# Decoder layer on one core: ternary thresholds two batches later, first layer norm one batch earlier

## The reference, cut to what matters

```python
x = layernorm(x + attn(x, Wq, Wk, Wv, Wo))         # x: 16 batches x 112 tokens x 256
x = layernorm(x + xattn(x, ctx, Wq, Wk, Wv, Wout)) # ctx: 16 x 375 keys x 192, 8 heads of 128
x = layernorm(x + ffn(x, W1, b1, W2, b2))          # width 1024

def xattn(x, context, ...):      # each head: 1792 queries against all 6000 keys
    softmax(q @ k.T * 1.5 * 128 ** -0.5) @ v, then @ Wout + bout

def ternary(w):                                    # on W1 and W2, for ffn
    scale = maximum(mean(abs(w)), 1e-8)
    return clip(round(w / scale), -1, 1)
```

## Time and profile before

| | us |
|---|---|
| median of 3 executions | 2416.77 (2416.18 to 2417.38) |
| the profiled execution | 2416.18, its span 2414.4 |
| PE busy | 2301.5 (95%) |
| DVE busy | 2037.4 (84%) |
| ACT busy | 1870.8 (77%) |
| POOL busy | 1850.6 (77%) |

### The profile page before, as it was taken

How to read it: one execution, slowest core, us unless ns; L and a number is a source line. 1 busy time by engine, 2 the same in 40 slices (tenths; PEclk the granted TensorE clock), 3 DMA queues, 4 the chain that set the end, 5 groups by cost and what they waited for, 6 DMA issues and landing times. The chain is left out here.

```text
span 2414.4 us, 67945 instructions
## 1 busy us (share of the span) xinstructions
PE 2301.5 (95%) x28874; PEld 2050.6 (85%) x28874; DVE 2037.4 (84%) x2237; ACT 1870.8 (77%) x2181; POOL 1850.6 (77%) x1092
## 2 busy tenths in 40 slices
PE   7988999999999999999989999999999999999787
PEld 3447998899889998999879988999899988998774
DVE  7778888888888888888878888888888888888777
ACT  4246888788888888888878888888888888888535
POOL 8733888788878887888878887889788888899201
PEclk9999999999999999999999999999999999999999
DMA  6401000000000000000000000000000000011211
GB/s 200 144 19 32 4 7 13 4 7 6 11 6 4 7 13 4 6 6 4 13 4 6 6 11 6 6 4 13 4 6 6 4 6 6 4 43 46 72 47 30
DMA packets 34869, 50.80 MB, mean 21 GB/s; under 512 B 2352, under 2 KB 27408, under 8 KB 34576
## 3 DMA queue, kind: packets, MB, share of 16 engines
q1 hardware_dynamic: 34576, 46.54, 6.6%
HBM read 31.01 MB, written 15.52 MB: 19 GB/s over the span
## 5 line engine op out<-in xcount | busy, mean ns | idle before, releaser
L1189 POOL TENSOR_TENSOR e_lo<-ring,e_hi 128x1024 f16<-128x1024 f32 (+1 forms) x665 | 1384.4, 2099 | 182.4 <-ACT ring L709 156.1
L847 DVE TENSOR_TENSOR run_max<-psum,run_max 128x1024 f16<-128x1024 f32 (+1 forms) x616 | 738.5, 1199 | 267.5 <-ACT ring L692 267.1
L692 ACT ACTIVATE ring<-psum 128x1024 f32<-128x1024 f32 (+1 forms) x672 | 674.0, 1003 | 228.4 <-PE psum L398 147.2
L868 DVE SCALAR_TENSOR_TENSOR ring<-ring,psum 128x1024 f32<-128x1024 f32 (+1 forms) x672 | 794.2, 1188 | 8.3 <-PE psum L630 8.3
L398 PE MATMUL psum<-qx_hi,k_hi 128*128 128x256 f16 x2632 | 719.1, 273 | 6.9 <-DVE run_max L847 6.8
L422 PE MATMUL psum<-v_main,e_hi 128*128 128x129 f16 x4032 | 718.7, 220 | 6.3 <-POOL e_lo L1189 6.3
L398 PE MATMUL psum<-qx_hi,k_lo 128*128 128x256 f16 x2632 | 718.9, 273 | 2.2 <-issue 2.2
L424 PE MATMUL psum<-v_main,e_hi 128*128 128x128 f16 x4032 | 719.2, 222 | 0.0
L398 PE MATMUL psum<-qx_lo,k_hi 128*128 128x256 f16 x2632 | 718.8, 273 | 0.0
L426 PE MATMUL psum<-v_main,e_lo 128*128 128x129 f16 x4032 | 717.2, 219 | 0.0
L709 ACT ACTIVATE ring<-ring 128x1024 f32<-128x1024 f32 (+1 forms) x672 | 695.7, 1035 | 1.3
(11 more groups left out here) (196 smaller groups left out, 2846.3 us busy)
## 6 DMA issues: line engine op xcount, KB each, us to landing
o_scratch<-o_buf SPq DMA_DIRECT2D x56, 129.0 KB, 2.7
raw<-o_scratch SPq DMA_DIRECT2D x16, 451.5 KB, 3.6
stage<-in_ctxT SPq DMA_DIRECT2D x6, 500.0 KB, 3.9
stage<-in_ctxT SPq DMA_DIRECT2D x12, 250.0 KB, 4.7
w_scratch<-wall SPq DMA_DIRECT2D x1, 2304.0 KB, 10.8
wall<-w_scratch SPq DMA_DIRECT2D x6, 384.0 KB, 3.9
x<-in_xT SPq DMA_DIRECT2D x4, 448.0 KB, 6.4
res<-in_x SPq DMA_DIRECT2D x1, 1792.0 KB, 15.0
```

Source lines behind the costliest of these rows:

```text
L692: a.activation(ring[:, f % SLOTS, 0:n], pair(f)[:, 0:n], ACT.Copy).then_inc(s_kept, 1)
L847: ins = v.tensor_tensor(run_max[:, 0:n], pair(f)[:, 0:n], run_max[:, 0:n], ALU.max)
L868: v.scalar_tensor_tensor(slot, slot, LIFT, psum[:, 6, 0:QB].unsqueeze(1).broadcast_to([P, t, QB]), ALU.add, ALU.subtract).then_inc(s_sub, 1)
L1189: g.tensor_tensor(e_lo[f % NEL][:, 0:n], slot, e_hi[f % NEH][:, 0:n], ALU.subtract).then_inc(s_lo, 1)
```

## The change

The thresholds' inputs are summed in iterations 6 and 8 instead of 5 and 6. PE's sum over the partitions goes from iteration 6 to 8, and the thresholds go from the beginning of iteration 7 to the end of iteration 9, just ahead of the first `statistics`. Statistics and roots go one iteration forward (from 10, 12, 14 to 9, 11, 13), as do the pairs of norms and the two query pieces. Batches 10 and 11 are normalised in iteration 15 and no more in the run-up, where batches 12 to 15 are left, in steps 2 to 5. In step 1, ACT's roots stand ahead of the norm's f16 half.

```diff
-        SUMS = {5: 0, 6: 1}
+        SUMS = {6: 0, 8: 1}
...
-        NORMS = {11: (0, 1), 12: (2, 3), 13: (4, 5), 14: (6, 7), 15: (8, 9)}
-        STATS = {10: 0, 12: 1, 14: 2}
+        NORMS = {10: (0, 1), 11: (2, 3), 12: (4, 5), 13: (6, 7), 14: (8, 9), 15: (10, 11)}
+        STATS = {9: 0, 11: 1, 13: 2}
...
-        START[13] += [("q", 0)]
-        START[14] += [("q", 1)]
+        START[12] += [("q", 0)]
+        START[13] += [("q", 1)]
...
-        LATE_NORMS = {i: i + 9 for i in range(1, 7)}
+        LATE_NORMS = {2: 12, 3: 13, 4: 14, 5: 15}
...  (PE)
-                        if b == 6:
+                        if b == 8:
                             pe.wait_ge(s_abs, 9)
                             pe.matmul(psum[:, 6, 0:8], lhsT=ones[:, :], rhs=sum_p[:, :],
...  (ACT, run-up)
+                    if f + LEAD == 1:
+                        roots(3)
                     if f + LEAD in LATE_NORMS:
                         norm_high(LATE_NORMS[f + LEAD])
-                    if f + LEAD == 1:
-                        roots(3)
...  (DVE)
-                        if b == 7:
-                            thresholds()
                         if b - 1 in STATS:
                             inverse(STATS[b - 1])
...
                         if b in SUMS:
                             weight_sums(SUMS[b])
+                        if b == 9:
+                            thresholds()
                         if b in STATS:
                             statistics(STATS[b])
...  (DVE, run-up)
                     if f + LEAD == 0:
-                        norm(10)
-                        norm(11)
                         residual(NB - 1)
                         statistics(3)
+                    elif f + LEAD == 1:
+                        inverse(3)
+                        norm(12)
+                        norm(13)
                     elif f + LEAD in LATE_NORMS:
                         norm_low(LATE_NORMS[f + LEAD])
-                        if f + LEAD == 1:
-                            inverse(3)
```

## The result

| | before | changed |
|---|---|---|
| median | 2416.47 (2415.30 to 2417.38, 4 executions) | 2433.67 (2432.32 to 2435.71, 4 executions) |
| ratio | | 1.0073, 95% interval 1.0054 to 1.0090 |
| span of the profiled execution | 2414.4 | 2432.0 |
| POOL's ternary weights start | 104.37 | 126.28 |
| last RECIPROCAL (L955) of the self-attention | 182.91 | 201.11 |

The changed kernel is slower by 17.2 us. The predicted 2432.5 us lie 16.0 us above this median of the kernel before, and the sum of steps was 15.7. The spans differ by 17.6 us. At the last RECIPROCAL the difference is already 18.2, and little is added or given back later.

The account below looks back on a forecast made before the run. Until 183 us no engine is full, short waits pass from engine to engine; afterwards PE is busy and only shifts. +16.3 - 0.6 = +15.7 us on 2416.18 gives 2431.9, median 2432.5, range 2428 to 2436.5.

Parts of the forecast that it names:

- Thresholds and POOL's start: Thresholds follow iteration 9's L965 at 123.5, so POOL's ternary weights start at 124.3, 19.9 us later than before.
- the pair of W2's sum and PE's reduction: Moved from iteration 6 to 8, same pieces at the same cost: 0, with 0.3 us allowed either way.
- Statistics: L974 in iteration 9 waits for POOL's first ternary instruction, until 129.75; bounds 0.17 and 5.3 us.
- The new wait: Iteration 11: DVE reaches batch 2's norm at 144.0 and stands 11.5 us for batch 0's keep, until 155.5.
- the balance: At batch 2's norm: 13.4 us to spare, less 4.9 for arriving earlier, less 19.9 for POOL's later start.
- the locks rival: Norms of batches 0 and 1 wait for POOL instructions; arrival after 155.5 adds up to 3 us: 2435.5, chance 0.08.
- The rest of iteration 11: From PE's transpose of batch 2 to iteration 12's first maximum: 7.07 us at low clock, 4.33 without that.
- the rival in which it costs nothing: PE is at full clock at once after the stall, iteration 11 ends after 4.33 us: +13.0, 2429.8, chance 0.10.
- Iterations 12 to 15: RECIPROCAL distances 9.55, 9.80, 8.45 and 6.5 us, one iteration more than before; last RECIPROCAL at 199.2, +16.3.
- Run-up: After the last RECIPROCAL, two norms leave DVE and two pairs of transposes leave PE: -0.6 us, bounds 0 and -1.5.
- The sum: Whole kernel: +16.3 at the last RECIPROCAL less 0.6 for the run-up gives +15.7 us, median 2432.5.

Follow-up runs that it names:

- The second profile of the changed kernel: The changed kernel, unaltered, timed again on the chip of a later run: 2435.11 us against 2417.58 for the kernel before, ratio 1.0070.
- With the clock held: Changed kernel plus 50 (second run: 40) unused matmuls on PE in iteration 11's idle time: 2429.23 us, ratio 1.0050 (2429.54, 1.0043).

## Why the prediction was right

*Thresholds and POOL's start: right, 2.0 us too early.* 124.3 was predicted, 126.28 came. Of this, 1.5 are the pair of W2's sum and PE's reduction: from that sum to the next RECIPROCAL it was 7.92 us before and 9.46 after. Another 0.3 is the start of the span (first RECIPROCAL 57.24 and 57.55). PE's wait was as long (3.63 before, 3.71 after), but the clock stayed low longer behind it: PE's windows of the changed kernel have 0.50 from 114 to 120 us, those of the kernel before only from 100 to 102 and 0.73 in the next. The order of the instructions alone doesn't decide this. The second profile of the changed kernel (DVE's timeline) has 7.92 again:

```profile
112.30 2.45 DVE L1009 TENSOR_REDUCE sum_p<-w 128x1 f32<-128x512 f32 x4
...
120.22 1.56 DVE L955 RECIPROCAL rden<-psum 128x224 f32<-128x224 f32 x1 [0.91 <-PE psum L501]
```

Its POOL starts at 125.83, and less the 1.5 us by which its first RECIPROCAL comes later (58.70) that is the predicted 124.3. I had costed this pair at 0 with 0.3 either way. In one execution of the kernel that was right, in the other it was 1.5 too little: the bound was too narrow, since the clock makes the same code cost more or less from execution to execution. Over this pair, from RECIPROCAL to RECIPROCAL, it is 12.2 to 12.3 us in all four profiles that have it in iteration 6 as before. In the six that have it in iteration 8 it is 12.7 in two and 14.3 in four, so the new place does have a part in it.

*Statistics: right.* L974 takes 5.34 us, the whole POOL instruction of about 5.3 that the prediction let it wait for.

*The new wait: right in its place and its end, with the balance shared otherwise.* The keep comes at the end of the six instructions, batch 2's norm at 157.43 against 155.5 predicted (2.0 of which is POOL's start). DVE stood 8.6 us there and not 11.5, because it arrived at 148.8 and not 144.0. 2.0 of these 4.8 us are again POOL's start, the rest is that the norms of batches 0 and 1 had waited for POOL's instructions (7.41 us). That was the first half of the locks rival, and as computed there it changed nothing, since the arrival stayed in front of 155.5. The runs showed how close both are: with the wait for the keep removed, the kernel still stood at +13.0 us of +17.2.

The Trainium skill (SBUF — State Buffer, section "Who interferes with whom") says that a DVE `tensor_scalar` can take the port pair shared with POOL, and the later of the two then waits for a whole instruction. The traces agree wherever L974 or a norm came up beside a ternary instruction: the wait ends with POOL's (151.15 + 4.05 = 155.20 and 155.34). The exception is the norm that passed between two of them, in two runs: with the thresholds at the end of iteration 8 (a pair of 2.96 us), and with the thresholds late and the norms as before (a pair of 2.20).

*The rest of iteration 11: too dear by 1.2 us here.* 7.07 was predicted, 5.92 measured (158.28 to 164.20), and 6.87 in the second profile of the same kernel. With the clock held it is 4.27, so the clock is worth 1.6 to 2.6 us, and the rival in which it costs nothing is refuted. The Trainium skill (TensorE: Matmul & The Clock Gate, section "HAM oscillation — how this bites in real kernels") says that a wait for data in the middle of a kernel makes the next matmuls start at the low clock; the rows at 0.50 behind 152 us agree.

*Iterations 12 to 15: right, with two errors of opposite sign.* The distances of the RECIPROCALs were predicted as 9.55, 9.80, 8.45 and 6.5; DVE's timeline of the changed kernel has 9.55, 9.79, 7.61 and 8.04:

```profile
166.12 1.56 DVE L955 RECIPROCAL rden<-psum 128x224 f32<-128x224 f32 x1
175.67 1.56 DVE L955 RECIPROCAL rden<-psum 128x224 f32<-128x224 f32 x1 [0.59 <-PE psum L501]
185.46 1.56 DVE L955 RECIPROCAL rden<-psum 128x224 f32<-128x224 f32 x1
193.07 1.56 DVE L955 RECIPROCAL rden<-psum 128x224 f32<-128x224 f32 x1 [1.32 <-PE psum L501]
201.11 1.56 DVE L955 RECIPROCAL rden<-psum 128x224 f32<-128x224 f32 x1 [0.71 <-PE psum L501]
```

The 8.45 was 0.8 too dear. I had taken it from a distance in which PE makes the four products L462 for the next batch. In front of iteration 15's RECIPROCAL there are none: from L483 to L501 pass 0.50 us there (190.79 to 191.29), and 1.26 with them (162.83 to 164.09).

The last distance has two values in the profiles: 6.36 with full clock, and 7.98 to 8.04 where the clock falls in front of iteration 15's projection. PE's timelines show what stands in front of it, first in the kernel before, then in the changed kernel, then in the second profile of the changed kernel:

```profile
177.28 0.41 PE L520 MATMUL psum<-ident,rows 112*128 112x112 f32 x2 [2.44 <-DVE rows L986]
```

```profile
195.44 0.45 PE L520 MATMUL psum<-ident,rows 112*128 112x112 f32 x2 [1.45 <-DVE rows L986]
```

```profile
195.96 0.41 PE L520 MATMUL psum<-ident,rows 112*128 112x112 f32 x2 [1.44 <-DVE rows L986]
```

In the six profiles with the old order of norms the wait is 2.44 us and the distance 7.98 to 8.04 every time. In the seven with the new order the wait is 1.44 or 1.45, and the distance is 6.36 in five and 7.99 or 8.04 in two. So the prediction read this place right: the wait for the root goes, and the slow clock mostly goes with it. The first profile of the changed kernel (8.04) is one of the two exceptions, its second (6.36) isn't.

*Run-up: right in sign.* -0.6 was predicted, -0.24 measured (18.20 at the last RECIPROCAL, 17.96 at the first `e_lo`).

*The sum: its closeness is in part luck.* In the profile the steps are off by +2.3 us (the transpose of batch 2, 158.28 against 155.95), -1.2, -0.8, +1.5 and +0.4, which leaves about +2.3 (17.96 against 15.7). Three of them were off by more than 1 us.

The claim behind it all, that delayed thresholds are the cause and the moved norms only the amplifier, was tested from both sides. Thresholds alone cost 9.2 us at the last RECIPROCAL (192.11 against 182.91), norms alone 1.8 (184.67), both 18.2. Counted from the first RECIPROCAL it is 10.3, 0.5 and 17.9, or 15.6 in the second profile of the changed kernel. What is left over, 5 to 7 us, fits the iteration by which the first waiting norm stands earlier (43.68 against 35.95 us behind it).

What stays open is why 40 more instructions in front remove a stop at PE's loop turn. That additional instructions on PE do it, far from the place and without any work to win, is shown, and the stops go with the loading of instructions. Whether it hangs on the number, on an alignment, or on something else was not tried. A norm in a form that isn't locked out by POOL wasn't tried either; it would show the order's own worth without locks.

## What to carry to other kernels

An engine that waits long isn't free to be started later: follow what stands behind its block of work, and subtract. Here 13.4 us of slack met 21.9 of delay and one iteration of advance. Where a wait is removed, look which second wait ends at the same moment; here the locks held DVE until 155.34 us, and the keep would have held it until about 156. And before a difference of 1 or 2 us between two profiles is believed, compare a landmark that stands ahead of the change: here it alone moved by up to 2.7 us.

## What the runs showed of the hardware that I had not expected

- DVE's norm from SBUF to SBUF (112 x 256 f32, two per-partition operands) takes about 0.40 us alone, and up to 4214 ns beside a POOL instruction, the longest of 16 in the changed kernel. POOL's ternary instructions lose at most 0.16 us (5.60 against 5.44).
- 40 matmuls of 8 columns at the beginning of the program, in idle time, make the whole faster by 4.6 us (2412.74 against 2417.31). In the profiles the gain is in one block 1.25 ms later, where PE stops once and not twice while instructions are loaded.
- Behind a wait of 3.71 us PE came back to 2.4 GHz about 7 us after its first instruction in one execution of the changed kernel, and about 4 us after it in another. Behind a wait of 1.44 or 1.45 us the clock fell in two of seven executions; behind one of 2.44 us it fell in six of six.
